# Causal attention beside a gated FFN: scores computed once with two heads in row tiles, bias and maximum fused, weights turned by DMA

## The reference

```python
xn = _layernorm(x)
qkv = xn @ W_attn + b_attn                        # q, k, v: 16 heads of 64
att = einsum('bqhd,bkhd->bhqk', q, k) / 8 / temperature
att = att + slopes[h] * (key - query)             # ALiBi
att = where(key <= query, att, -inf)              # causal
y = einsum('bhqk,bkhd->bqhd', softmax(att), v)
h = silu(xn @ wg.T) * (xn @ wu.T)                 # wg, wu, wd: int8 range / 127
out = x + y @ W_proj + b_proj + h @ wd.T
```

## Time and profile before

| what | value |
|---|---|
| time, median of 3 runs | 1129.7 us (1129.56 to 1129.7) |
| profiled execution, span of the core read here | 1127.7 us |
| spans of the eight cores | 1122.9 to 1127.7 us |
| busy PE / VectorE / ScalarE / GpSimd | 1080.2 / 630.7 / 478.3 / 333.0 us |
| TensorE clock granted over the span | 0.997 |
| DMA moved | 98.34 MB |

### The profile page before, as it was taken

How to read it: one execution, slowest core, us unless ns; L and a number is a source line. 1 busy time by engine, 2 the same in 40 slices (tenths; PEclk the granted TensorE clock), 3 DMA queues, 4 the chain that set the end, 5 groups by cost and what they waited for, 6 DMA issues and landing times.

```text
span 1127.7 us, 23969 instructions; the slowest of 8 cores (1122.9 to 1127.7 us)
## 1 busy us (share of the span) xinstructions
PE 1080.2 (96%) x7270; PEld 536.0 (48%) x7270; DVE 630.7 (56%) x1254; ACT 478.3 (42%) x869; POOL 333.0 (30%) x529
## 2 busy tenths in 40 slices
PE   2898899999999999999999999999999999999998
PEld 1444355555555545555454554555554344444443
DVE  4631877777776787777777778677873100111000
ACT  2353355655564555565565556556666200000000
POOL 7210213332332333333233233223343422222220
PEclk9999999999999999999999999999999999999999
DMA  8449051443351533144332113113622652525221
GB/s 191 140 98 169 21 86 33 91 73 69 63 101 30 87 74 67 39 85 72 69 56 54 43 43 67 30 38 67 174 62 56 204 185 75 187 75 187 76 80 69
DMA packets 57070, 98.34 MB, mean 87 GB/s; under 512 B 23292, under 2 KB 43909, under 8 KB 55862
## 3 DMA queue, kind: packets, MB, share of 16 engines
q0 software_dynamic: 7872, 35.66, 17.5%
q1 hardware_dynamic: 46178, 52.65, 16.4%
q10 hardware_dynamic: 2900, 8.51, 1.9%
HBM read 90.50 MB, written 27.26 MB: 104 GB/s over the span
## 4 chain that ended last, share of the span: by engine, by line
PE 88%; DVE 4%; issue 3%; DMA 2%; ACT 1%; POOL 1%; ACTq 0%; DVEq 0%; POOLq 0%; SPq 0%
PE ps_gu L806 26%; PE ps_dn L968 15%; PE ps_s L897 10%; PE ps_t L878 10%; PE ps_m L786 9%; PE ps_y L916 5%; PE ps_dn L963 5%; PE ps_t L846 5%; DVE cm L631 2%; DMA xstage<-xin 1%; PE ps_s L900 1%; DMA tile_s<-tiles 1%; DVE hst L567 1%; POOL gs_s L503 1%; DVE st L579 0%
## 5 line engine op out<-in xcount | busy, mean ns | idle before, releaser
L631 DVE TENSOR_REDUCE cm<-ps_s 128x1 f32<-128x512 f32 (+3 forms) x640 | 377.1, 607 | 127.7 <-PE ps_s L897 75.8
L748 ACT ACTIVATE pt<-ps_t 128x512 bf16<-128x512 f32 (+1 forms) x576 | 327.8, 575 | 279.2 <-PE ps_t L878 268.5
L806 PE MATMUL ps_gu<-xnT,wubuf 128*128 128x512 bf16 x768 | 258.9, 378 | 2.4 <-DVE hst L567 2.3
L806 PE MATMUL ps_gu<-xnT,wgbuf 128*128 128x512 bf16 x768 | 259.6, 378 | 1.2 <-ACT kst L692 1.2
L897 PE MATMUL ps_s<-kx,qx 67*128 67x512 bf16 (+3 forms) x640 | 215.3, 347 | 10.8 <-DVE cm L631 8.2
L878 PE MATMUL ps_t<-qx,kx 104*128 104x512 bf16 (+3 forms) x640 | 212.6, 348 | 1.9 <-DVE qx L661 1.0
L968 PE MATMUL ps_dn<-wdres,hb 128*128 128x512 bf16 x768 | 168.5, 379 | 0.0
L497 POOL TENSOR_SCALAR th_s<-th_s 128x512 f32<-128x512 f32 x96 | 59.4, 619 | 359.6 <-ACT th_s L700 359.4
L916 PEld LDWEIGHTS ps_y<-Vt,pt 128*128 128x128 bf16 x2176 | 121.5, 97 | 78.9
L681 DVE SCALAR_TENSOR_TENSOR outsb<-ps_dn,xres 128x512 f32<-128x512 f32 x32 | 20.7, 687 | 205.1 <-PE ps_dn L968 205.1
L916 PE MATMUL ps_y<-Vt,pt 128*128 128x65 bf16 x2176 | 134.2, 193 | 0.0
(11 more groups left out here) (75 smaller groups left out, 710.0 us busy)
## 6 DMA issues: line engine op xcount, KB each, us to landing
h_sc<-hst SPq DMA_DIRECT2D x96, 128.0 KB, 1.7
hb<-h_sc SPq DMA_DIRECT2D x4, 3072.0 KB, 15.0
xstage<-xin SPq DMA_DIRECT2D x16, 512.0 KB, 4.5
xres<-xin POOLq DMA_DIRECT2D x16, 512.0 KB, 4.9
out<-outsb ACTq DMA_DIRECT2D x15, 512.0 KB, 2.7
wgbuf<-wg_r POOLq DMA_DIRECT2D x12, 512.0 KB, 7.3
wubuf<-wu_r POOLq DMA_DIRECT2D x12, 512.0 KB, 10.2
wd_sc<-wd_r POOLq DMA_DIRECT2D x12, 512.0 KB, 10.9
```

The source lines that it names most:

```text
L631: e.tensor_reduce(cm[:, c0:c0 + 1], ps_s[:, s % 2 * 512:s % 2 * 512 + w], AX.X, AluOpType.max, negate=True).then_inc(sem["v_mx"], 1)
L748: e.activation(pt[t % NPT][:, 0:w], ps_t[:, t % 2 * 512:t % 2 * 512 + w], AF.Exp).then_inc(sem["a_e"], 1)
L806: mm = e.matmul(ps_gu[:, r // 8 * 512:r // 8 * 512 + 512], w[:, w0:w0 + 128], xnT[:, dc * T + tb * 512:dc * T + tb * 512 + 512], start=(dc ...
```

## The change

The scores of a head are computed once, with queries on partitions. A unit is now a pair of heads p and a pair of query tiles, 15 - j and j, so that each unit has 17 blocks of 128x128 a head. It has three batches: the first 1024 keys of tile 15 - j, the rest of its keys, and the keys of tile j. q and k stay where the projection puts them (one head of the pair on partitions 0 to 63, the other on 64 to 127), q is scaled by 1/slope, and the bias is a ramp of integers in SBUF that also holds the causal mask. One VectorE instruction adds the ramp to the scores, multiplies by -slope, writes them to SBUF as f32 (sc), and takes the minimum, which is the negated maximum; a second small instruction writes that minimum. ScalarE takes the exponential of a whole row of tiles, with the maximum as its bias, and SyncE turns the weights by three transposing DMAs a unit. The value product runs two units later (LAG = 2). The V and Y tensors share memory (VY); y is transposed once per pair, 16 blocks at a time. q's evacuation moves from VectorE to ScalarE. Of the 12 loads of wdres 4 instead of 8 go ahead of the loop's end. The core of the diff:

```diff
-    for n in range(4 * H):
-        b = n % 4
-        for i in range(4):
-            for c in range(b):
-                out.append((n, i, c * 512, 512, c))
...
+def batch_of(k):
+    n, b = divmod(k, 3)
+    j = unit_of(n)[2]
+    if b == 0:
+        return n, 15 - j, 0, 1024
+    if b == 1:
+        return n, 15 - j, 1024, (8 - j) * 128
+    return n, j, 0, (j + 1) * 128
...
+def rows_at(k):
+    n, b = divmod(k, 3)
+    n -= LAG
+    if n < 0 or n >= NU:
+        return []
+    return [[(n, 0)], [(n, 1), (n, 2), (n, 3)], []][b]
...
-            ps_s = s4.enter_context(nc.psum_tensor("ps_s", [128, 1024], F32))
-            ps_t = s4.enter_context(nc.psum_tensor("ps_t", [128, 1024], F32))
+            ps_s = s4.enter_context(nc.psum_tensor("ps_s", [128, 2048], F32))
...
+            def turn(n, r, blocks):
+                _, _, b0, _ = row(n, r)
+                e.dma_start_transpose(
+                    out=pt[n % 2][:, b0 * 128:(b0 + blocks) * 128].rearrange("p (k q) -> p k q", q=128),
+                    in_=pr[n % 2][:, b0 * 128:(b0 + blocks) * 128]).then_inc(
+                        sem[f"l_t{'abs'[r]}{n % 2}"], 16)
...
+            def biased(k):
+                n, i, c0, w = batch_of(k)
+                p, _, j = unit_of(n)
+                b = k % 3
+                wide = (i + 1) * 128
+                for g in range(2):
+                    e.wait_ge(sem["p_s"], 2 * k + g + 1)
...
+                    if n and b < 2:
+                        e.wait_ge(sem["a_e"], 4 * (n - 1) + 2 * b + g + 1)
...
+                    e.tensor_tensor_reduce(scores(n, g + (2 if b == 2 else 0), c0, w),
+                                           ps_s[:, g * 1024:g * 1024 + w],
+                                           ramp[:, T - wide + c0:T - wide + c0 + w], -slope[2 * p + g], start,
+                                           AluOpType.add, AluOpType.min, cm[:, at:at + 1]).then_inc(
+                                               sem["v_mx"], 1)
...
+            def weights(n, r):
...
+                e.activation(pr[n % 2][:, b0 * 128:(b0 + blocks) * 128], scores(n, r, 0, blocks * 128), AF.Exp,
+                             bias=cm[:, at:at + 1], scale=-1.0).then_inc(sem["a_e"], 1)
...
+            def score_batch(k):
+                n, i, c0, w = batch_of(k)
+                p = n // 8
+                if k:
+                    e.wait_ge(sem["v_mx"], 2 * k)
...
+                for o in range(0, w, 512):
+                    wo = min(512, w - o)
+                    for g in range(2):
+                        mm = e.matmul(ps_s[:, g * 1024 + o:g * 1024 + o + wo],
+                                      qst[p % 2][64 * g:64 * g + 64, i * 128:(i + 1) * 128],
+                                      kst[p % 2][64 * g:64 * g + 64, c0 + o:c0 + o + wo], start=True, stop=True)
...
+            def weighted(n, r):
...
+                if r < 3:
+                    e.wait_ge(sem[f"l_t{'abs'[r]}{n % 2}"], 16 * (n // 2 + 1))
...
+            for k in range(NST):
...
+                    score_batch(k)
...
+                gate_up(m0, mid)
+                for n, r in rows_at(k):
+                    weighted(n, r)
+                gate_up(mid, FM[k])
```

More of the change, by code:

```diff
@@ L23 @@
 NHP = H // 2
-KS = 67
-KT = 104
 VW = 65
-NPT = 8
-LEAD = 24
+VS = 16 * 2 * VW
+NU = 8 * NHP
+LAG = 2
 NF_ATT = 88
@@ L69, in key_groups @@
[L69 to L152, removed]
@@ L155, in gate_up_plan @@
[L155 to L180, removed]
-        dve += len(ended) * (op(4) + op(256))
-        ended = [a for a in A if lt[tg[a][0]] == a]
-        if M is not None and M[0] == "m":
-            pe += 128
-            dve += op(512)
[L186 to L189, removed]
-        lack.append(dve - pe)
-    lack = [sum(lack[max(0, k - 2):k + 3]) / len(lack[max(0, k - 2):k + 3]) for k in range(len(lack))]
-    total = NF_ATT * 16 * 512
@@ new lines, in qk_at, with gate_up_plan @@
+def qk_at(k):
+    n, b = divmod(k, 3)
+    p, x, _ = unit_of(n)
+    return (p + 1, x) if b == 0 and n < NU - 8 else None
+def gate_up_plan():
+    room = []
+    for k in range(NST):
+        if k < NSB:
+            t = 2 * (295 + 1.06 * batch_of(k)[3])
+        else:
+            t = 1500.0
+        for n, r in rows_at(k):
+            j = unit_of(n)[2]
+            t -= 30 * ((16 - j) if r < 2 else (j + 1))
+        if qk_at(k) is not None:
+            t -= 8 * 216
+        room.append(t)
+    total = NF_ATT * 16 * 216
@@ L196, in gate_up_plan @@
         mid = (lo + hi) / 2
-        if sum(max(0.0, x + mid) for x in lack) < total:
+        if sum(max(0.0, x + mid) for x in room) < total:
             lo = mid
@@ L201, in gate_up_plan @@
     done, out = 0.0, []
-    for x in lack:
-        done += (max(0.0, x + hi) + total / len(lack)) / 2
-        out.append(min(NF_ATT * 16, int(done / 512 + 0.5)))
+    for x in room:
+        done += max(0.0, x + hi)
+        out.append(min(NF_ATT * 16, int(done / 216 + 0.5)))
     out[-1] = NF_ATT * 16
@@ L260, in build_program @@
         xnT = sb(st, "xnT", [128, DC * T], BF16)
+        with contextlib.ExitStack() as s8:
+            outsb = [sb(s8, f"outsb{i}", [128, C], F32) for i in range(2)]
         wgbuf = [sb(st, f"wgbuf{i}", [128, 2048], BF16) for i in range(2)]
@@ L666, in _ @@
+            for k in range(NST):
+                if k < NSB:
+                    biased(k)
+                if k % 3 == 1 and k // 3 >= LAG:
+                    normalised(k // 3 - LAG)
                 for f in units_ended(k, 15):
@@ new lines, in _ @@
+            evac_k0(NTB - 1)
+            def weights(n, r):
+                _, _, b0, blocks = row(n, r)
+                at = n % 2 * 6 + 2 + r
+                e.wait_ge(sem["v_mx"], 6 * n + r + 3)
+                if r == 0 and n >= 2:
+                    for x in "abs":
+                        e.wait_ge(sem[f"l_t{x}{n % 2}"], 16 * (n // 2))
+                e.activation(pr[n % 2][:, b0 * 128:(b0 + blocks) * 128], scores(n, r, 0, blocks * 128), AF.Exp,
+                             bias=cm[:, at:at + 1], scale=-1.0).then_inc(sem["a_e"], 1)
@@ L750, in _ @@
+            for k in range(NST):
+                if k < NSB and qk_at(k) is not None:
+                    if k == 0:
+                        e.wait_ge(sem["v_cbq"], 2)
+                    evac_qk(*qk_at(k))
                 for f in units_ended(k, 7):
                     tanh_gate(f)
-                if M is None:
-                    continue
-                if M[0] == "qk" and M[2] and M[1] % 2:
-                    evac_k(M[1] // 8 + 1, M[1] % 8 // 2)
+                if k < NSB and k % 3:
+                    for r in range(2):
+                        weights(k // 3, r + (0 if k % 3 == 1 else 2))
```

519 lines of the change are left out of this document (190 added, 329 removed), and 2 rows, old and new, of the table SEMS.

## The result

| | before | after |
|---|---|---|
| median of the runs | 1129.7 us | 1045.8 us |
| runs | 1129.56 to 1129.81 | 1044.08, 1045.8, 1047.43 |
| ratio, 95% | | 0.926, 0.924 to 0.927 |
| profiled run, its span | 1127.7 span | 1045.8, span 1044.2 |

The change makes the kernel faster by 84 us, of the 120 that were forecast. One more run, at 1103.9 us, fell in a disturbed state of the chip, and it is left out of the median, as are the runs of this kind in the experiments. The 1046 us lie inside the range, but in the third rival's (1040 to 1100), just above the forecast's own (975 to 1045).

The account below looks back on a forecast made before the run. PE bounds attention before; after, the PE-VectorE loop over one score buffer: 576 + 12 + 15 + 31 = 634 us. 1129.7 - 753.8 + 634 = 1009.9, so 1010 us (975 to 1045; whole range 930 to 1100).

Parts of the forecast that it names:

- third rival: Attention: transposes set the end, 552 + 127 us of other transfers = 679; 1055 us in all (1040 to 1100), chance 0.20.
- The transposes: Attention, SyncE's queue: 2304 blocks in 200 transfers plus stores, 552 us, 8.6 a unit against 9.0; nothing added.
- A delay of one unit (9 us) is absorbed: Attention: weights are used two units after their scores, so a transpose one unit late adds nothing.
- The loop: Attention: VectorE and PE alternate over one score buffer; 576 + 12 + 15 + 31 = 634 us for the stretch.
- the turns of VectorE: Attention: VectorE stands while PE computes a score batch, 0.5 to 0.7 us, three times a unit, 1.9 us.
- lower end, 349: Attention, VectorE's score reduces: if the second small instruction hides, 349 us remain; 405 was taken.
- Row tiles: Attention scores on PE: two heads side by side; entering and leaving costs at most 63 us, 31 taken.
- rival 2: Attention scores: the pair's matmuls run one after the other, 634 + 30 us in the stretch, 1040 in all; chance 0.10.
- The tail: After attention: 261 us as before, no wait for wdres or hb; nothing added, cover 13 us.
- Rivals 4: Attention: better overlap, gate products and normalisation vanish in VectorE's turns, stretch 560 us; 936 in all (905 to 965), chance 0.13.
- rival 5: Attention: transposes wait for their slowest engine; at 0.307 us a block 826 us, 1202 in all; chance 0.10.
- 6: Attention: the reduce with bias makes two passes, 290 us more on VectorE, 1300 in all; chance 0.05.

Follow-up runs that it names:

- The first experiment: Changed kernel without the 192 transposing transfers of the exponentials; the value product reads them unturned (y differs): 980.9 us, ratio 0.868.
- experiments 12: Changed kernel with half of the blocks turned and only the first two pairs of gate and up loads made (y and h differ): 994.2 us, ratio 0.880.
- experiments 2: Changed kernel with half of the blocks turned, each used twice, in as many transfers (y differs): 1007.8 us, ratio 0.894.
- 3: Changed kernel with gate and up weights loaded only for the first two chunks, all transposes kept (h differs): 1012.2 us, ratio 0.896.

## Why the prediction was right or wrong

**Direction and size.** Faster was right; 1010 was forecast and 1046 measured. The third rival's sum, 552 + 127 = 679 us of transfers in the stretch, comes nearest to the measured 667. That is in part luck: its 552 are the time of SyncE's queue, 119 us of gaps and stores among them, and not time of the engines. The errors in order:

- **The transposes, the step that failed.** The prediction summed them against SyncE's queue alone, 552 us or 8.6 a unit against 9.0, and wrote "nothing is added here". It did so although its own row put 127 us of other transfers on the same 16 engines. For the queue alone the sum was nearly right: SyncE's queue stood idle for 86 of the 667 us, most of it for the exponentials, so it was in use for 581, where 552 were forecast.

```profile
SPq L294 <- ACT pr L606: 75.1, 27, 44.0
```

  On the engines, which the forecast didn't sum, the records show 462 us of blocks + 67 of other transfers in the hardware queue + 143 of casting loads = 672. A block took 0.212 us of data, not 0.188, the casting loads 143 instead of 127, and transposing packets lasted 26.4 ns in the mean where before had 22.0. A sign of being wrong that it named came, value products that waited for transposes for more than 20 us: 50.7. And 25 of the 192 transfers, of whatever size, took over 4 us in SyncE's queue, five of them over 10. The first experiment prices the whole at 66 us of the stretch, where the sum had nothing.
- **Absorbing a delay.** "A delay of one unit (9 us) is absorbed" held for the median landing (4.7 us) but not for the longest (21.8); before had already shown 12.5. And the price per stall includes the clock, which the prediction left at its 1.00.
- **The loop.** Forecast 634, measured 601 with the transposes away. That it is near is in part luck, since errors of both signs cancel. Too high were the reduces, 405 us. All their instructions together hold VectorE for 344.8 us in the first experiment (L480 there):

```profile
115.70:717.10 601.40, 344.77 (x768) 1.00 0.31 65
```

```profile
403.57 1.22 DVE L480 CUSTOM_DVE_ANT_0 sc<-ps_s,ramp 128x1024 f32<-128x1024 f32 x1 [1.45 <-PE ps_s L723]
404.73 0.08 DVE L480 DVE_READ_ACCUMULATOR2_ANT cm<- 128x1 f32 x1
404.73 1.22 DVE L480 CUSTOM_DVE_ANT_0 sc<-ps_s,ramp 128x1024 f32<-128x1024 f32 x1
```

  The second instruction starts together with the next reduce and adds nothing, which is the prediction's lower end, 349. In the changed kernel, by shape:

```profile
L491 DVE CUSTOM_DVE_ANT_0 sc<-ps_s,ramp 128x1024 f32<-128x1024 f32 x144 | 170.7, 1221 | 54.7 <-PE ps_s L735 39.3 <-ACT pr L606 14.9
...
L491 DVE DVE_READ_ACCUMULATOR2_ANT cm<- 128x1 f32 x384 | 32.0, 83 | 0.0
...
L491 DVE CUSTOM_DVE_ANT_0 sc<-ps_s,ramp,cm 128x1024 f32<-128x1024 f32 x16 | 19.9, 1282 | 8.0 <-PE ps_s L735 7.9 <-issue 0.2
```

  The reduce of 1024 columns is 1221 ns, as "1.22" said, so one pass; the second instruction is 83 ns and not 145. Too high were the turns of VectorE as well, 93.6 us in the first experiment (0.49 each for 192 batches), where 1.9 a unit, 122 us, was set. Too low were the gate products and normalisations. Half of them, 49 us, were to add; they hold VectorE for 430.8 - 344.8 = 86 us beside those turns. And 15 us were set for waits of the gate products, where VectorE waits 43.6 us for GpSimd's product and 15.2 for ScalarE to free sc:

```profile
DVE sc L480 <- PE ps_s L723: 93.6, 104, 2.6
DVE hst L423 <- POOL gs_s L366: 43.6, 26, 3.5
DVE sc L480 <- ACT pr L594: 15.2, 14, 1.9
```

  345 + 86 + 94 + 44 + 15 = 584; the last 17 us to 601 are smaller gaps and the last steps.
- **Row tiles.** Side by side was right, rival 2 wrong. In the first experiment entry took about 0.10 and exit 0.11 us a batch (402.23 to 402.76 to 403.30, less 2 x 0.216 each time), an estimated 192 x 0.2 = 38 us on PE, for the 31 taken and the bound of 63. How much of it falls into PE's waits for VectorE no run shows. PE opens the stretch in the changed kernel the same way, 0.54 us to the next group:

```profile
111.04 0.61 PE L735 MATMUL ps_s<-kst,qst 64*128 64x512 bf16 x4 [1.03 <-ACT kst L541]
111.58 1.90 PE L649 MATMUL ps_m<-xnT,wqk_b 128*128 128x512 bf16 x8
```

- **The Trainium skill's two sentences.** The Trainium skill's drain between tiling modes and its parallel tiles (TensorEngine Tiling (Array Packing), Key Properties) agree with the 0.2 us and with the 0.54 us. The Trainium skill's statement that transposing transfers run as fast as plain ones (Advanced Engine Details and Errata, X-Bar Transpose (TRN2)) doesn't: the 71.3 MB turned from pr would be an estimated 204 us by it, and the engines' records have 462.
- **The tail.** "Nothing is added" for wdres was off by 4.7 us, 265.8 against 261.1. SyncE's queue at the end of attention:

```profile
775.39 5.27 SPq L319 DMA_DIRECT2D wdres<-wd_sc  x8
780.75 0.88 SPq L279 DMA_DIRECT2D h_sc<-hst  x2
781.72 9.54 SPq L306 DMA_TRANSPOSE VY<-ysb  x1
791.35 0.98 SPq L279 DMA_DIRECT2D h_sc<-hst  x2
```

  The 4 MB of wdres themselves were in time. But the last transpose of y stands behind them for 9.54 us (2.13 is the median of the eight such transfers), and the stores of h behind that. VectorE, then PE:

```profile
791.08 0.69 DVE L434 SCALAR_TENSOR_TENSOR hst<-ps_gu,gs_s 128x512 bf16<-128x512 f32 x1 [5.21 <-DMA h_sc<-hst]
```

```profile
791.91 2.64 PE L669 MATMUL ps_gu<-xnT,wubuf 128*128 128x512 bf16 x8 [2.28 <-DVE hst L434]
```

  VectorE waits 5.21 us for a store to free its buffer and PE 2.28 for VectorE; eight matmuls then take 2.64 instead of 1.89 us. The prediction asked when wdres is needed, and not what is queued behind it.
- **Rivals 4, 5 and 6.** Not met: no full overlap even without transposes (601, not 560); stretched blocks, 0.212 and not the 0.307 of rival 5; one pass on VectorE.

The sum therefore reads: forecast 634 - 33 (loop) + 66 (transfers) = 667, and + 4.7 in the tail, less 1.7 in the prologue and 0.4 in what lies around the span: 1009.9 + 33.3 + 4.7 - 1.7 - 0.4 = 1045.8.

**Open.** Whether late transposes come from the engines' load or from the queue that issues them in order; what the last 13 us between experiments 12 and 1 are; what pairs one after the other would cost; and what makes single transposes take over 10 us, since neither the packets' length nor the loads' spacing changed it.

## What to carry to other kernels

Sum the transfers on the DMA engines, all queues together and with what runs there already, before asking whether one queue has time for them; a share near 1, as here, is a warning. A share below 1 is no all-clear, as the experiments 2, 3 and 12 show: look at the longest landing against the cover, not at the median. And when work moves to engines with free time, as the turns did to PE and ScalarE, look at the buffer over which they exchange it.
